# Layer kernel, first batch: weights signal apart, the identity loads alone, GpSimd takes low parts and constants, loads in another order

## The chip, the cores and the metric

One core of one Trainium2 chip runs the kernel. The metric is the device time of one execution in microseconds. The engines are TensorE (PE, with its weight loads as PEld), VectorE (DVE), ScalarE (ACT), GpSimd (POOL) and SyncE (SP), which here only issues DMAs. They run apart and are held together by semaphores.

## The reference, cut to what matters

```python
xn = layernorm(x)                                  # x: 16 x 512 x 256
q, k, v = feature(xn@Wq+bq), feature(xn@Wk+bk), xn@Wv+bv     # elu + 1, 16 heads of 16
kv  = einsum('bkhd,bkhm->bhdm', k, v)
out = einsum('bqhd,bhdm->bqhm', q, kv) / max(sum(q * sum(k)), 1e-6)
attn = out @ Wo + bo
shared = swiglu(xn @ w_in.T) @ w_out.T
g = softmax(xn @ wg.T + gb); e = softmax(masked(xn @ we.T + eb)); top 2 of 8 experts
h = swiglu(xn @ w1.T)
routed = sum over the chosen e of weight[e] * h @ w2[e].T
return x + attn + shared + routed
```

## The kernel before

The program handles the 16 sequences of 512 rows one after the other ("batches"; the first and the last are written out, the 14 between are a hardware loop), and then multiplies the rows, sorted by their pair of experts, with the expert weights. A batch is held transposed as xnT. The order of work on every engine is the order of the code; there is no scheduler.

To keep 32-bit accuracy on an engine that multiplies rounded fp32r numbers, every operand is kept as a high part (rounded to fp32r) and a low part (the rest), and each product is three matmuls (`mm3`: high by high, high by low, low by high). In the first batch all weights must be loaded and split: `high_parts` on ScalarE casts a staged weight and counts `w_round`; `low_parts` on VectorE, or `low_part` and `in_low` on GpSimd, subtracts. VectorE splits W_k, the router's W_r, W_v and W_q and counts `w_split`; GpSimd splits W_in (four times `in_low`, counted by `ffn_split`), the two halves of W_1 (`w1_split`) and W_out. `kv_w_ld` counts the landings of W_k, W_r and W_v together. The staging buffers are kb (W_k, W_v), relut (W_r, then the constants `c_round`), hrow (W_q), res and phiq (W_in), wstage and gated (W_1).

What happens before the first batch's products: VectorE takes the statistics of x, GpSimd the root (`reciprocal_root`, tile rstd), VectorE normalises into hrow (`first_normalise`), TensorE transposes with the identity, which is the first 128 columns of the constant block `c_stay`, ScalarE rounds (`first_high`, xnT_hi) and VectorE subtracts (`first_low`, xnT_lo). TensorE has run 64 matmuls on a constant tile before that (`warm_up`). Then come the constants on VectorE (nbq, triones, spread, run, tok; semaphore `const_set`).

In a batch TensorE does for each of four row tiles the key and router product (6 matmuls) and the value product (6), then the query product, `hidden(0)` (shared expert, chunk 0), the key-value sums, `hidden(1)`, `routed(0)`, ranks, normaliser sums (these need phiq), `routed(1)` to `routed(3)`, the spread of the reciprocals (they need `rdiag`, kept in qn_hi), `hidden(2)`, `hidden(3)` and the output products. VectorE's part: `k_in` adds the key's bias, `phi_k` the feature map, `logits_in`, `probabilities`, `best_two` the routing, then phiq (which in the first batch waits for `ffn_split` to reach 4, since phiq is W_in's staging buffer), `gate(0)`, `gate(1)`, ranks, row tables, reciprocals. In the first batch `stats_in(1)` and `norm_out(1)`, the next batch's statistics, stand among the `k_in`. ScalarE's part: value copies, exponentials, W_1's casts, the query's activations, `silu(0)`, `second_normalise`, W_out's cast, `high(0)` (h_hi), `silu(1)`.

Of the kernel before, what the change touches and what calls it, by code (L numbers as in the profile page):

```python
# [6 lines left out]
def layer_program(nc, x, w_k, w_v, w_q, w_o, w_in, w_out, w_exp, w_rt, b_q, b_kl, b_o,  # L7
# [41 lines left out]
    with ctx:  # L49
# [145 lines left out]
        kv_w_ld = sem("kv_w_ld")  # L195
# [5 lines left out]
        x0_ld = [sem(f"x0_ld{t}") for t in range(TB)]  # L201
        stay_ld = sem("stay_ld")
        c_ld = sem("c_ld")
# [5 lines left out]
        w_split = sem("w_split")  # L209
# [156 lines left out]
        def _(sp):  # L366
# [92 lines left out]
        def _(pe):  # L459
            def first_transposes():  # L460

                pe.wait_ge(stay_ld, 16)
# [33 lines left out]
            def batch(b, last):  # L496

                for t in range(TB):
# [9 lines left out]
                    if first_row(b) and t == 0:  # L508
                        pe.wait_ge(w_split, 2)
# [8 lines left out]
                if first_row(b):  # L518
                    pe.wait_ge(w_split, 3)
# [7 lines left out]
                if first_row(b):  # L527
                    pe.wait_ge(ffn_split, 1)
                    pe.wait_ge(const_set, 1)
# [22 lines left out]

                pe.wait_ge(oh_rdy, b + 1)
# [83 lines left out]
            pe.wait_ge(w_split, 1)  # L637
# [42 lines left out]
        def _(act):  # L680
# [39 lines left out]
            def batch(b, last):  # L720
                if first_row(b):
                    act.wait_ge(w_split, 3)
                    act.wait_ge(const_set, 1)
# [17 lines left out]
                if first_row(b):  # L741
                    act.wait_ge(w1_ld[1], 16)
# [39 lines left out]
            for buf, of, _, _ in stage_kv[1:3]:  # L782
                act.dma_start(buf, of).then_inc(kv_w_ld, 16)
            act.wait_ge(kv_w_ld, 16 * 3)
            high_parts(stage_kv)
# [41 lines left out]
        def _(dve):  # L827
# [155 lines left out]
            def batch(b, last):  # L983
# [153 lines left out]
            def low_parts(stage, n):  # L1137
# [4 lines left out]
                ins.then_inc(w_split, 1)  # L1142
# [21 lines left out]
            low_parts(stage_kv[2:3], 2)  # L1164
            low_parts(stage_q, len(stage_kv))
            dve.wait_ge(c_ld, 16 * 3)
# [250 lines left out]
```

## Time and profile before

| | |
|---|---|
| median of 3 runs | 915.67 us (915.26 to 917.14) |
| the profiled execution, its own time | 917.56 us |
| its span, first to last instruction | 915.6 us |
| TensorE busy | 898.0 us, 98% |
| VectorE / ScalarE / GpSimd busy | 76% / 40% / 44% |
| TensorE's granted clock, mean over the span | 0.993 |

The span lies inside the execution's time; 1.96 us lie around it. A granted clock of 1.00 is TensorE at full speed, 2.4 GHz, and 0.50 at half. Busy times of matmuls overlap a little, as they are pipelined. Times in the rows are counted from the span's start. An "idle before" with an arrow tells how long the engine had stood and what released it.

### The profile page before, as it was taken

Reading aid. Unit: us, or ns where it says so; the run is one execution under the profiler, and the core shown is the slowest. Engines: PE = TensorE matmul, PEld = TensorE weight load, DVE = VectorE, ACT = ScalarE, POOL = GpSimd, SP = SyncE. Lnnn points to the kernel's source line nnn. Section 1 sums busy time; section 2 is a strip of 40 time slices with the busy share of each in tenths; the row PEclk is TensorE's granted clock in tenths of the full one; section 3 lists DMA queues with packets and bytes.
Section 4 is the critical chain, followed back from the end, with each engine's and each line's share of the span. In section 5 each row is a group of like instructions: output and inputs, shape, how many; then the busy total and the mean of one; then the engine's idle time right before and its main releaser. Section 6 shows DMA issues by size and latency. Waiting matters only on the chain. (4 is left out here: it accounts for less than half of the span.)

```text
span 915.6 us, 22781 instructions
## 1 busy us (share of the span) xinstructions
PE 898.0 (98%) x6982; PEld 810.8 (89%) x6983; DVE 694.0 (76%) x1816; ACT 367.3 (40%) x605; POOL 404.0 (44%) x486
## 2 busy tenths in 40 slices
PE   8899999999999999999999999999999999999996
PEld 7698988889898989898898989898988999999996
DVE  6978777787868687877878786878685777777774
ACT  4654534353535445344535354453531222222220
POOL 3654342433434244434343342534341655665554
PEclk9999999999999999999999999999999999999998
DMA  6432414131323323141313233232156888888870
GB/s 215 132 123 70 126 47 126 69 103 70 105 91 102 123 72 117 55 126 69 103 69 103 92 103 109 85 109 65 59 197 140 141 140 144 146 141 150 140 132 1
DMA packets 141992, 98.63 MB, mean 108 GB/s; under 512 B 53136, under 2 KB 133008, under 8 KB 141968
## 3 DMA queue, kind: packets, MB, share of 16 engines
q1 hardware_dynamic: 103584, 62.50, 24.1%
q0 software_dynamic: 15920, 25.32, 12.3%
q10 hardware_dynamic: 22464, 10.51, 5.1%
q8 instruction: 13, 0.21, 0.1%
q14 instruction: 11, 0.09, 0.0%
HBM read 53.29 MB, written 46.43 MB: 109 GB/s over the span
## 5 line engine op out<-in xcount | busy, mean ns | idle before, releaser
L1232 POOL TENSOR_TENSOR h_lo<-gated,h_hi 128x256 fp32r<-128x256 f32 x128 | 98.8, 793 | 139.9 <-ACT h_hi L714 139.9
L355 PE MATMUL bank<-xnT_hi,win_hi 128*128 128x512 f32 x256 | 102.1, 399 | 0.0
L355 PE MATMUL bank<-wone_hi,xnT_hi 128*128 128x512 f32 x256 | 101.5, 397 | 0.2 <-DVE relut L1035 0.2
L356 PE MATMUL bank<-xnT_lo,win_hi 128*128 128x512 f32 x256 | 100.4, 392 | 0.0
L357 PE MATMUL bank<-wone_hi,xnT_lo 128*128 128x512 f32 x256 | 99.7, 390 | 0.0
L356 PE MATMUL bank<-wone_lo,xnT_hi 128*128 128x512 f32 x256 | 99.6, 389 | 0.0
L357 PE MATMUL bank<-xnT_hi,win_lo 128*128 128x512 f32 x256 | 99.6, 389 | 0.0
L1256 POOL TENSOR_TENSOR res<-res,bo_t 128x256 f32<-128x256 f32 x64 | 47.3, 769 | 112.9 <-DMA res<-x 112.9
L1251 POOL DMA_INDIRECT h_d<-hrow,pos_i x64 | 63.1, 986 | 72.8 <-DVE hrow L981 38.3
L355 PE MATMUL bank<-wexp_hi,xnT_hi 128*128 x304 | 85.6, 282 | 2.0 <-DVE xnT_lo L1154 2.0
L356 PE MATMUL bank<-wexp_lo,xnT_hi 128*128 x304 | 85.8, 282 | 0.0
L357 PE MATMUL bank<-wexp_hi,xnT_lo 128*128 x304 | 85.6, 282 | 0.0
L356 PE MATMUL bank<-wexp_lo,h_hi 128*128 x296 | 82.9, 280 | 0.0
L355 PE MATMUL bank<-wexp_hi,h_hi 128*128 x296 | 82.6, 279 | 0.0
L357 PE MATMUL bank<-wexp_hi,h_lo 128*128 x296 | 82.6, 279 | 0.0
L714 ACT CAST h_hi<-gated 128x512 fp32r<-128x512 f32 x64 | 39.7, 621 | 101.3 <-DVE gated L977 101.3
L977 DVE TENSOR_TENSOR gated<-gated,bank 128x512 f32<-128x512 f32 x64 | 43.9, 685 | 47.3 <-ACT gated L710 47.3
L1329 POOL DMA_INDIRECT out<-res,idx_cur x39 | 62.0, 1590 | 36.7 <-DVE res L1183 24.8
L355 PE MATMUL bank<-wout_hi,h_hi 128*128 128x256 f32 x256 | 71.9, 281 | 0.0
L357 PE MATMUL bank<-wout_hi,h_lo 128*128 128x256 f32 x256 | 71.5, 279 | 0.0
L356 PE MATMUL bank<-wout_lo,h_hi 128*128 128x256 f32 x256 | 71.4, 279 | 0.0
L718 ACT ACTIVATE hrow<-bank 128x512 f32<-128x512 f32 x64 | 38.1, 597 | 80.0 <-PE bank L357 80.0
(204 smaller groups left out, 2700.4 us busy)
## 6 DMA issues: line engine op xcount, KB each, us to landing
res<-x SPq DMA_DIRECT2D x16, 512.0 KB, 3.7
out<-res SPq DMA_DIRECT2D x16, 512.0 KB, 2.8
xt<-x SPq DMA_DIRECT2D x15, 512.0 KB, 3.4
xn_d<-xt SPq DMA_DIRECT2D x15, 512.0 KB, 4.9
xt<-xn_d SPq DMA_DIRECT2D x60, 128.0 KB, 2.7
xt<-h_d SPq DMA_DIRECT2D x76, 64.0 KB
xt<-h_d ACTq DMA_DIRECT2D x76, 64.0 KB
kb<-h_d SPq DMA_DIRECT2D x76, 64.0 KB
```

What stands on the lines that cost most here:

```text
L355: e.matmul(to, w_hi, m_hi_, start=first_, stop=False, skip_group_check=free)
L356: e.matmul(to, w_hi, m_lo_, start=False, stop=False, skip_group_check=free)
L357: return e.matmul(to, w_lo, m_hi_, start=False, stop=last_, skip_group_check=free)
L714: act.copy(h_hi[:, j, :], gated[:, j % 2, :]).then_inc(hhi_rdy, 1)
L718: act.activation(hs[t], bank[gate_bank][:, :], ACT.Silu).then_inc(rsil_rdy, 1)
L977: dve.tensor_tensor(gated[:, j % 2, :], gated[:, j % 2, :], bank[up_bank][:, :], ALU.mult).then_inc(gate_rdy, 1)
L1232: ins = pool.tensor_tensor(h_lo[:, j, cols], gated[:, j % 2, cols], h_hi[:, j, cols].bitcast(f32), ALU.subtract)
L1251: pool.indirect_dma_start(d, bass.IndirectOffsetOnAxis(ap=pos_i[:, t:t + 1], axis=0), src, None).then_inc(done, 16)
L1256: ins = pool.tensor_tensor(res[:, t, :], res[:, t, :], bo, ALU.add)
L1329: pool.indirect_dma_start(out, bass.IndirectOffsetOnAxis(ap=idx_cur[:, t // TB, t % TB:t % TB + 1], axis=0), ring[t], None, bounds_check=N ...
```

## The change

Signals: `kv_w_ld` becomes `k_w_ld`, `rt_w_ld` and `v_w_ld`, and ScalarE waits before each cast for its own weight. `w_split` becomes `k_split`, `v_split` and `q_split`. The identity is a load of its own (64 KB, `ident_ld`) in the place of `c_stay`; the other columns follow later.

VectorE subtracts W_k's low part before it normalises, W_r's after. GpSimd subtracts W_v's and W_q's low parts, in halves of 128x256, and makes the five constants, all ahead of W_in's. Its second root now comes behind both halves of W_1.

SyncE waits for the third tile of x before it issues W_q and what follows, and for W_in's landing before it issues W_1. `b_kl` and `b_q` have a signal of their own (`b_ld`). The waits for `const_set` move to later places on TensorE, ScalarE and VectorE. VectorE's `stats_in(1)` comes after the fourth `k_in` instead of the third, and the third waits for `v_split`.

```diff
-            loads(kv_w_ld, [], stage_kv[0:1])
-            sp.dma_start(stay[:, :], c_stay).then_inc(stay_ld, 16)
+            loads(k_w_ld, [], stage_kv[0:1])
+            sp.dma_start(ident, c_stay[:, 0:P]).then_inc(ident_ld, 16)
+            sp.wait_ge(x0_ld[2], 16)
             loads(q_w_ld, [], stage_q)
-            loads(c_ld, [(bkl[:, :], b_kl), (bq[:, :], b_q)], [])
+            loads(b_ld, [(bkl[:, :], b_kl), (bq[:, :], b_q)], [])
+            sp.dma_start(stay[:, P:], c_stay[:, P:]).then_inc(stay_ld, 16)
             loads(in_w_ld, [], stage_in)
...
             sp.dma_start(xt[:, :, :], x_rows(1)).then_inc(x_ld, 16)
+            sp.wait_ge(in_w_ld, 16 * 2)
             for n in range(2):
                 loads(w1_ld[n], [], stage_w1[n:n + 1])
...
-            act.wait_ge(kv_w_ld, 16 * 3)
-            high_parts(stage_kv)
+            for n, done in enumerate((k_w_ld, rt_w_ld, v_w_ld)):
+                act.wait_ge(done, 16)
+                high_parts(stage_kv[n:n + 1])
...
                 for t in range(TB):
+                    if first_row(b) and t == 2:
+                        dve.wait_ge(v_split, 1)
                     k_in(t)
-                    if first_row(b) and t == 2:
+                    if first_row(b) and t == 3:
                         stats_in(1)
-                    if first_row(b) and t == 3:
                         norm_out(1, True)
+                        dve.wait_ge(const_set, 1)
...
             norm(0)
+            low_parts(stage_kv[0:1], 0)
             first_normalise()
-            low_parts(stage_kv[0:2], 0)
+            low_parts(stage_kv[1:2], 1)
             first_low()
...
+            for buf, _, hi, lo, n, done in ((*stage_kv[2], 3, v_split), (*stage_q[0], 4, q_split)):
+                pool.wait_ge(w_round, n)
+                for c in range(DC):
+                    ins = pool.tensor_tensor(lo[:, c, :], buf[:, c, :], hi[:, c, :].bitcast(f32), ALU.subtract)
+                ins.then_inc(done, 1)
+            pool.wait_ge(b_ld, 16 * 2)
+            pool.wait_ge(stay_ld, 16)
...
+            pool.wait_ge(c_ld, 16)
+            pool.tensor_copy(triones[:, 0, :], tri_f)
+            pool.tensor_copy(spread[:, :, :], spread_f).then_inc(const_set, 1)
...
-                if n == 0:
-                    reciprocal_root(1)
+            reciprocal_root(1)
```

GpSimd from the first root to the second, before (win is W_in, wone is W_1):

```order
L1226 TENSOR_TENSOR rstd<-var,mhalf 128x4 [waits var_rdy,pool_set]
L1300 TENSOR_TENSOR win_lo<-res,win_hi 128x128 [waits w_round]
L1300 TENSOR_TENSOR win_lo<-res,win_hi 128x128
L1300 TENSOR_TENSOR win_lo<-phiq,win_hi 128x128 x2
L1300 TENSOR_TENSOR win_lo<-res,win_hi 128x128 x2
L1300 TENSOR_TENSOR win_lo<-phiq,win_hi 128x128 x2
L1291 TENSOR_TENSOR wone_lo<-wstage,wone_hi 128x256 [waits w_round]
L1291 TENSOR_TENSOR wone_lo<-wstage,wone_hi 128x256 x3
L1226 TENSOR_TENSOR rstd<-var,mhalf 128x4 [waits var_rdy]
L1291 TENSOR_TENSOR wone_lo<-gated,wone_hi 128x256 [waits w_round]
L1291 TENSOR_TENSOR wone_lo<-gated,wone_hi 128x256 x3
L1300 TENSOR_TENSOR win_lo<-res,win_hi 128x128 x2
```

And now, the start of the same stretch:

```order
L1231 TENSOR_TENSOR rstd<-var,mhalf 128x4 [waits var_rdy,pool_set]
L1302 TENSOR_TENSOR wv_lo<-kb,wv_hi 128x256 [waits w_round]
L1302 TENSOR_TENSOR wv_lo<-kb,wv_hi 128x256
L1302 TENSOR_TENSOR wq_lo<-hrow,wq_hi 128x256 [waits w_round]
L1302 TENSOR_TENSOR wq_lo<-hrow,wq_hi 128x256
L1306 TENSOR_SCALAR nbq<-bq 128x2 [waits stay_ld,b_ld]
L1307 COPY run<-stay 128x32
L1308 COPY tok<-stay 128x4
L1310 CAST triones<-relut 128x128 [waits c_ld]
L1311 CAST spread<-relut 128x256
L1319 TENSOR_TENSOR win_lo<-res,win_hi 128x128 [waits w_round]
```

Eight instructions for W_v, W_q and constants stand ahead of W_in's low parts, and the constants wait for three loads. The end of the stretch now:

```order
L1296 TENSOR_TENSOR wone_lo<-wstage,wone_hi 128x256 [waits w_round]
L1296 TENSOR_TENSOR wone_lo<-wstage,wone_hi 128x256 x3
L1296 TENSOR_TENSOR wone_lo<-gated,wone_hi 128x256 [waits w_round]
L1296 TENSOR_TENSOR wone_lo<-gated,wone_hi 128x256 x3
L1231 TENSOR_TENSOR rstd<-var,mhalf 128x4 [waits var_rdy]
L1319 TENSOR_TENSOR win_lo<-res,win_hi 128x128 x2
L1319 TENSOR_TENSOR win_lo<-phiq,win_hi 128x128 x2
```

The root has moved behind the second half of W_1, to just ahead of W_in's last two `in_low`.

VectorE from the variance to the constants, before:

```order
L861 TENSOR_SCALAR var<-mv 128x4 [waits v_link]
L870 TENSOR_SCALAR hrow<-xt,mv,rstd 128x256 [waits rstd_rdy]
L870 TENSOR_SCALAR hrow<-xt,mv,rstd 128x256 x3
L1141 TENSOR_TENSOR wk_lo<-kb,wk_hi 128x2x256 [waits w_round]
L1141 TENSOR_TENSOR wk_lo<-relut,wk_hi 128x2x10 [waits w_round]
L883 TENSOR_TENSOR xnT_lo<-bank,xnT_hi 128x512 [waits thi] x2
L1141 TENSOR_TENSOR wv_lo<-kb,wv_hi 128x512 [waits w_round]
L1141 TENSOR_TENSOR wq_lo<-hrow,wq_hi 128x512 [waits w_round]
L1169 TENSOR_SCALAR nbq<-bq 128x2 [waits stay_ld,kv_w_ld,c_ld]
L1170 CAST triones<-relut 128x128
L1171 CAST spread<-relut 128x256
```

And now, down to the first `k_in` (kb):

```order
L872 TENSOR_SCALAR var<-mv 128x4 [waits v_link]
L1154 TENSOR_TENSOR wk_lo<-kb,wk_hi 128x2x256 [waits w_round]
L881 TENSOR_SCALAR hrow<-xt,mv,rstd 128x256 [waits rstd_rdy]
L881 TENSOR_SCALAR hrow<-xt,mv,rstd 128x256 x3
L1154 TENSOR_TENSOR wk_lo<-relut,wk_hi 128x2x10 [waits w_round]
L894 TENSOR_TENSOR xnT_lo<-bank,xnT_hi 128x512 [waits thi] x2
L999 TENSOR_TENSOR kb<-bank,bkl 128x256 [waits stay_ld,k_done,b_ld,k_split]
```

W_k's low part has moved ahead of the normalisation, and W_v, W_q and the constants are gone from the engine. VectorE around the second statistics, before:

```order
L988 TENSOR_TENSOR kb<-bank,bkl 128x256 [waits k_done]
L989 TENSOR_TENSOR lg<-bank,bkl 128x10
L988 TENSOR_TENSOR kb<-bank,bkl 128x256 [waits k_done]
L989 TENSOR_TENSOR lg<-bank,bkl 128x10
L850 BN_STATS stats<-xt 128x6 [waits x_ld]
L850 BN_STATS stats<-xt 128x6 x3
L988 TENSOR_TENSOR kb<-bank,bkl 128x256 [waits k_done,v_link]
L989 TENSOR_TENSOR lg<-bank,bkl 128x10
L857 BN_AGGR mv<-stats 128x2 x4
```

And now:

```order
L999 TENSOR_TENSOR kb<-bank,bkl 128x256 [waits k_done,v_split]
L1000 TENSOR_TENSOR lg<-bank,bkl 128x10
L999 TENSOR_TENSOR kb<-bank,bkl 128x256 [waits k_done]
L1000 TENSOR_TENSOR lg<-bank,bkl 128x10
L861 BN_STATS stats<-xt 128x6 [waits x_ld]
L861 BN_STATS stats<-xt 128x6 x3
L868 BN_AGGR mv<-stats 128x2 [waits v_link]
L868 BN_AGGR mv<-stats 128x2 x3
```

The four statistics stand behind the fourth key addition. SyncE's issues, before:

```order
L372 DMA kb<-w_k 128x512
L374 DMA stay<-c_stay 128x443
L372 DMA hrow<-w_q 128x512
L372 DMA bkl<-b_kl 128x266
L372 DMA bq<-b_q 128x2
L372 DMA res<-w_in 128x1024
L372 DMA phiq<-w_in 128x1024
L372 DMA relut<-c_round 128x384
L380 DMA xt<-x 128x4x256 [waits xn_rdy]
L372 DMA wstage<-w_exp 128x1024
```

And now:

```order
L378 DMA kb<-w_k 128x512
L380 DMA stay<-c_stay 128x128
L378 DMA hrow<-w_q 128x512 [waits x0_ld2]
L378 DMA bkl<-b_kl 128x266
L378 DMA bq<-b_q 128x2
L384 DMA stay<-c_stay 128x315
L378 DMA res<-w_in 128x1024
L378 DMA phiq<-w_in 128x1024
L378 DMA relut<-c_round 128x384
L388 DMA xt<-x 128x4x256 [waits xn_rdy]
L378 DMA wstage<-w_exp 128x1024 [waits in_w_ld]
L378 DMA gated<-w_exp 128x1024
```

The first load of `stay` is the identity, the second the rest; W_in (res, phiq) goes behind a wait and two more issues, W_1 behind a wait for W_in.

## Rows read from the trace of the kernel before

**Rows 1.** The page, part 1: busy us (share of the span) xinstructions.
```profile
PE 898.0 (98%) x6982; PEld 810.8 (89%) x6983; DVE 694.0 (76%) x1816; ACT 367.3 (40%) x605; POOL 404.0 (44%) x486
```

**Rows 2.** Windows: stretch, PE, PEld, DVE, ACT, POOL busy (x), PEclk, DMA share, GB/s.
```profile
10.70:11.88 1.18, 1.10 (x7) 0.91 (x7) 1.18 (x3) 0.21 (x1) 0.00 (x0) 0.88 1.02 381
...
14.00:15.00 1.00, 1.00 (x6) 1.00 (x6) 0.49 (x3) 0.74 (x1) 0.18 (x1) 0.50 1.02 414
15.00:16.00 1.00, 1.00 (x10) 1.00 (x9) 0.39 (x2) 0.20 (x1) 1.00 (x3) 1.00 0.98 374
...
40.00:60.00 20.00, 18.44 (x124) 16.58 (x123) 15.71 (x32) 5.98 (x10) 13.38 (x17) 1.00 0.28 100
```

**Rows 3.** Timeline, TensorE: start us, us, instruction, idle before and its releaser.
```profile
7.99 1.09 PE L466 MATMUL bank<-stay,hrow 128*128 128x128 f32 x8 [1.45 <-DMA stay<-c_stay]
...
10.78 0.36 PE L355 MATMUL bank<-wk_hi,xnT_hi 128*128 128x266 f32 x1 [1.70 <-DVE xnT_lo L883]
...
17.59 0.29 PE L357 MATMUL bank<-wk_hi,xnT_lo 128*128 128x266 f32 x1
...
31.41 0.64 PE L569 MATMUL bank<-phiq,khead 128*32 128x128 f32 x16 [0.73 <-DVE phiq L1022]
...
43.17 0.73 PE L593 MATMUL bank<-qn_hi,spread 128*128 128x512 f32 x2 [1.56 <-DVE qn_hi L1065]
```

**Rows 4.** Timeline, ScalarE: casts, and h_hi of the first hidden chunk.
```profile
8.18 0.62 ACT L683 CAST wk_hi<-kb 128x512 fp32r<-128x512 f32 x1 [4.26 <-DMA kb<-w_v]
...
12.75 1.04 ACT L683 CAST win_hi<-res 128x1024 fp32r<-128x1024 f32 x1 [1.84 <-DMA phiq<-w_in]
...
32.67 0.61 ACT L714 CAST h_hi<-gated 128x512 fp32r<-128x512 f32 x1
```

**Rows 5.** Timeline, VectorE, from normalising to gate 1.
```profile
6.67 1.38 DVE L870 TENSOR_SCALAR hrow<-xt,mv,rstd 128x256 f32<-128x256 f32 x4 [1.25 <-POOL rstd L1226]
...
9.94 1.29 DVE L883 TENSOR_TENSOR xnT_lo<-bank,xnT_hi 128x512 fp32r<-128x512 f32 x2 [0.33 <-ACT xnT_hi L688]
...
13.19 0.17 DVE L1169 TENSOR_SCALAR nbq<-bq 128x2 f32<-128x2 f32 x1 [0.77 <-DMA relut<-c_round]
...
16.46 0.42 DVE L988 TENSOR_TENSOR kb<-bank,bkl 128x256 f32<-128x256 f32 x1 [1.07 <-PE bank L357]
...
19.36 1.23 DVE L995 SCALAR_TENSOR_TENSOR hrow<-kb,hrow 128x512 f32<-128x512 f32 x1
...
29.52 1.29 DVE L1022 TENSOR_TENSOR phiq<-hrow,relut 128x512 f32<-128x512 f32 x2
...
31.22 0.68 DVE L977 TENSOR_TENSOR gated<-gated,bank 128x512 f32<-128x512 f32 x1
...
33.81 0.69 DVE L977 TENSOR_TENSOR gated<-gated,bank 128x512 f32<-128x512 f32 x1 [1.34 <-ACT gated L710]
```

**Rows 6.** Timeline, GpSimd, the weights' low parts and the second root.
```profile
14.82 0.88 POOL L1300 TENSOR_TENSOR win_lo<-res,win_hi 128x128 fp32r<-128x128 f32 x2 [8.18 <-ACT win_hi L683]
...
21.85 1.04 POOL L1226 TENSOR_TENSOR rstd<-var,mhalf 128x4 f32<-128x4 f32 x1
...
23.30 2.83 POOL L1291 TENSOR_TENSOR wone_lo<-gated,wone_hi 128x256 fp32r<-128x256 f32 x4 [0.41 <-ACT wone_hi L683]
...
28.60 0.88 POOL L1300 TENSOR_TENSOR win_lo<-phiq,win_hi 128x128 fp32r<-128x128 f32 x2
```

**Rows 7.** SyncE's issues from the timeline, then W_k's us to landing.
```profile
1.66 0.42 SPq L372 DMA_DIRECT2D kb<-w_k  x1
...
4.02 0.74 SPq L372 DMA_DIRECT2D res<-w_in  x1
...
kb<-w_k SPq DMA_DIRECT2D x1, 256.0 KB, 3.8
```

**Rows 8.** One line's instructions: duration ns min/median/max, first and last start.
```profile
L1141 DVE TENSOR_TENSOR wv_lo<-kb,wv_hi x1: 679/679/679, 11.1 to 11.1; 128x512 fp32r<-128x512 f32 x1
...
L1291 POOL TENSOR_TENSOR wone_lo<-wstage,wone_hi x4: 732/738/1179, 18.6 to 21.2; 128x256 fp32r<-128x256 f32 x4
```

More of the change, by code:

```diff
@@ L192, in layer_program @@
         bank = [ctx.enter_context(nc.psum_tensor(f"bank{i}", [P, 512], f32)) for i in range(8)]
-        kv_w_ld = sem("kv_w_ld")
+        k_w_ld = sem("k_w_ld")
+        rt_w_ld = sem("rt_w_ld")
+        v_w_ld = sem("v_w_ld")
         q_w_ld = sem("q_w_ld")
@@ L201, in layer_program @@
         x0_ld = [sem(f"x0_ld{t}") for t in range(TB)]
+        ident_ld = sem("ident_ld")
         stay_ld = sem("stay_ld")
+        b_ld = sem("b_ld")
         c_ld = sem("c_ld")
@@ L208, in layer_program @@
         w_round = sem("w_round")
-        w_split = sem("w_split")
+        k_split = sem("k_split")
+        v_split = sem("v_split")
+        q_split = sem("q_split")
         ffn_split = sem("ffn_split")
@@ L460, in first_transposes @@
             def first_transposes():
-                pe.wait_ge(stay_ld, 16)
+                pe.wait_ge(ident_ld, 16)
                 for t in range(TB):
@@ L508, in batch @@
                     if first_row(b) and t == 0:
-                        pe.wait_ge(w_split, 2)
+                        pe.wait_ge(v_split, 1)
                     if t == 2:
@@ L518, in batch @@
                 if first_row(b):
-                    pe.wait_ge(w_split, 3)
+                    pe.wait_ge(q_split, 1)
                 for o in range(DC):
@@ L528, in batch @@
                     pe.wait_ge(ffn_split, 1)
-                    pe.wait_ge(const_set, 1)
                 wait(pe, base_rdy, DC * b)
@@ L551, in batch @@
                 routed(0, (3, 4))
+                if first_row(b):
+                    pe.wait_ge(const_set, 1)
                 pe.wait_ge(oh_rdy, b + 1)
@@ L636, in _ @@
             first_transposes()
-            pe.wait_ge(w_split, 1)
+            pe.wait_ge(k_split, 2)
             rounds(pe, batch, B)
@@ L721, in batch @@
                 if first_row(b):
-                    act.wait_ge(w_split, 3)
-                    act.wait_ge(const_set, 1)
+                    act.wait_ge(q_split, 1)
                 for i in range(2):
@@ L741, in batch @@
                 if first_row(b):
+                    act.wait_ge(const_set, 1)
                     act.wait_ge(w1_ld[1], 16)
@@ L781, in _ @@
                 act.dma_start(xt[:, t, :], x[0, t * P:(t + 1) * P, :]).then_inc(x0_ld[t], 16)
-            for buf, of, _, _ in stage_kv[1:3]:
-                act.dma_start(buf, of).then_inc(kv_w_ld, 16)
-            act.wait_ge(kv_w_ld, 16 * 3)
-            high_parts(stage_kv)
+            for (buf, of, _, _), done in zip(stage_kv[1:3], (rt_w_ld, v_w_ld)):
+                act.dma_start(buf, of).then_inc(done, 16)
+            for n, done in enumerate((k_w_ld, rt_w_ld, v_w_ld)):
+                act.wait_ge(done, 16)
+                high_parts(stage_kv[n:n + 1])
             first_high()
@@ L1141, in low_parts @@
                     ins = dve.tensor_tensor(lo, buf, hi.bitcast(f32), ALU.subtract)
-                ins.then_inc(w_split, 1)
+                ins.then_inc(k_split, 1)
             def transposed(t, g):
@@ L1160, in _ @@
             norm(0)
+            low_parts(stage_kv[0:1], 0)
             first_normalise()
[L1162 removed]
+            low_parts(stage_kv[1:2], 1)
             first_low()
[L1164 to L1167 removed]
+            dve.wait_ge(k_split, 2)
+            dve.wait_ge(b_ld, 16 * 2)
             dve.wait_ge(stay_ld, 16)
[L1169 to L1175 removed]
             rounds(dve, batch, B)
@@ L1292, in low_part @@
                 ins.then_inc(done, 1)
+            for buf, _, hi, lo, n, done in ((*stage_kv[2], 3, v_split), (*stage_q[0], 4, q_split)):
[5 more added lines that the diff above has]
+            pool.wait_ge(stay_ld, 16)
+            pool.tensor_scalar(nbq[:, :], bq[:, :], -1.0, None, ALU.mult)
+            pool.tensor_copy(run[:, :], slot_row)
+            pool.tensor_copy(tok[:, :], tok0)
+            pool.wait_ge(c_ld, 16)
+            pool.tensor_copy(triones[:, 0, :], tri_f)
+            pool.tensor_copy(spread[:, :, :], spread_f).then_inc(const_set, 1)
             first = len(stage_kv) + len(stage_q)
```

8 lines of the change are left out of this document (removed).

## The prediction

> **What bounds the kernel now.** First the busy shares: TensorE is busy 898.0 of the 915.6 us, nothing else above 76% [rows 1]. So a change saves time only where TensorE stands or runs slowly. Next the windows over the first 60 us, where the change is, for TensorE's busy time and granted clock [rows 2]. From 10.70 to 11.88 us the clock averages 0.88, which is full speed followed by about 0.28 us at half, so it fell near 11.6. From 14 to 15 us it is still 0.50, the 1.2 GHz level, and from 15 us 1.00 again, 2.4 GHz. That is 3.4 us at half speed, a loss of 1.7 us. TensorE had stood 1.45 us before the transposes and 1.70 us before the first key product. From 40 to 60 us it misses 1.56 us, all before 43.17. TensorE's rows name its waits [rows 3]: the identity's load until 7.99, xnT_lo until 10.78, phiq until 31.41, rdiag (qn_hi) until 43.17, the last for 1.56.
>
> The other three engines tell what sets the last two. Read backwards: TensorE at 43.17 follows VectorE, which has had no idle time to speak of since gate 1 at 33.81. That waited 1.34 us for ScalarE's second silu, and before the silu stand, without a gap, its second normalisation, W_out's cast and h_hi (32.67) [rows 4, 5]. ScalarE's own chain began when VectorE's logits came, and these follow phi_k at 19.36 after an unbroken 2.90 us from the third key addition at 16.46 [rows 5]. Beside it runs GpSimd: low parts from 14.82 to 29.48, with one root between them at 21.85, and phiq starts at 29.52, as it waits for the last of them [rows 5, 6]. Two chains thus end together at phiq, and a third, ScalarE's, has 0.8 us of slack (gate 0, 1.7 us after phiq starts, is done at 31.9; h_hi runs at 32.67). TensorE's own earlier start is worth nothing until both yield.
>
> **The change part by part.** The sum goes against the profiled execution, 917.56 us (span 915.6); the runs' median, 915.67, is 1.89 us below it, and I carry differences over.
>
> 1. *Key low part ahead of normalising.* W_k is issued at 1.66 and lands 3.8 us later, 5.5 [rows 7]. The cast takes 0.62 [rows 4] and the subtraction 0.68, by the same form on W_v [rows 8]; they end near 6.85, and normalising started at 6.67 [rows 5]. Price: +0.2, last tile near 8.2 instead of 8.05.
> 2. *Identity alone, separate weight signals.* The transposes no longer wait for 221 KB; they follow the normalised tiles. The last two (0.14 each, 1.09 for eight [rows 3]) end near 8.55 instead of 9.08. ScalarE has its three casts behind it, since W_k, W_r and W_v no longer share one signal (it idled 4.26 us until 8.18 [rows 4]). So xnT_hi and then xnT_lo start 0.8 us earlier, 9.15 for 9.94, and the first key product at 10.0 for 10.78 [rows 3, 5]. Gain on TensorE: 0.8.
> 3. *W_v and W_q low parts to GpSimd.* A half (128x256) takes 0.74, so 1.5 us a matrix against 0.68 on VectorE [rows 8]. W_v: from about 7.6 to 9.1, wanted at 10.9. W_q: cast after xnT_hi, about 9.6 to 10.2; low part until 11.8, wanted after 15.8 at the earliest. Both cost nothing here. The Trainium skill ("GPSIMD Engine Reference", Engine selection) says that two-input elementwise work belongs on VectorE, GpSimd being about twice as slow. The rows agree (1.5 to 0.68), and the rule would price the move at 1.6 us, if GpSimd were not idle then; the trace shows it idle for 8.18 us before 14.82 [rows 6].
> 4. *Constants to GpSimd.* VectorE no longer waits for c_round until 13.19 [rows 5]. Of GpSimd's five instructions two wait for c_round, near 13.5, and none is larger than the 0.74 us form above, so they end by 15.0 at the latest. Nothing else on it is due before W_in's high parts, now 14.8 [rows 6]. Bounds: 0, and 1 us if c_round is that much later.
> 5. *Loads.* W_q, b_kl, b_q, the rest of c_stay and W_in leave after the third x tile has landed (about 4.0, an estimate), so that W_in, issued at 4.02 now [rows 7], goes about 1.9 us later. Bytes ahead of W_in's end are the same, and the DMA engines carry 381 and 414 GB/s in the windows around it [rows 2], so I move its landing from 12.7 [rows 4] only to 13.0; bounds: 12.4 (fewer transfers at once) and 14.6 (all 1.9 us kept). ScalarE's casts then end at 15.0. W_1's two loads, now behind W_in, land near 16.8 and 18 (3.4 to 3.9 us after W_in, an estimate from W_k's 3.8); ScalarE comes to the first near 16.8, so no cost.
> 6. *Stats after the fourth key addition.* phi_k(0) now comes one addition, four statistics and the aggregation (2.90 minus 0.45, 2.45 us) after the fourth key product, not 2.90 after the third. The 42 products up to there end at 17.88, 7.1 us after the first began, with the loss of 1.7 in them: 5.4 at full clock [rows 3].
> 7. *Root after both W_1 low parts.* The 1.04 us stood in a gap, as W_1's second high part was ready only 0.41 us after it [rows 6]. Now it stands on the chain to phiq. Price: up to 1.0.
>
> What the clock does decides. The idle time before the first key product falls from 1.70 to about 1.4 us and that before the transposes from 1.45 to 0.8, so I take it that the clock stays up, a little likelier than not. The Trainium skill ("TensorE: Matmul & The Clock Gate", HAM oscillation) has standing between bursts as the cause of the fall and warns that each costs the next burst. By that rule shorter gaps should spare the loss; where they still fall under it, the rival below holds. The trace shows one fall here and cannot say how near it was.
>
> *Clock stays up:* fourth key product at 10.0 + 5.4 = 15.4; phi_k(0) 17.85, 1.5 earlier. ScalarE's second W_1 cast ends 21.75. GpSimd: 15.0 + 3.4 (half of W_in, as from 26.1 to 29.48) + 3.1 = 21.5; then 21.8 + 2.83 + 1.04 + 3.4 = 29.1 [rows 6], so phiq 0.4 earlier. Gate 0 ends 31.5, h_hi runs at 31.5 for 32.67, and gate 1 at 32.65 for 33.81. Of 2.5 us on TensorE (0.8 + 1.7) 1.15 remain at 43.17; the rest stands as longer waits before phiq and rdiag. After that TensorE has no gap to give it back in, so it reaches the end.
>
> The runs may not have met the fall at all (they lie 1.89 below the profiled one). Without it the kernel before has phi_k(0) near 17.7 and phiq near 29.1 by the same working, so the gain would be nothing. Between 0 and 1.15 I take 0.6, 915.67 less 0.6: 915.1, with 914.3 to 915.8 as its own range.
>
> **The rivals.**
> *The clock falls again.* The fourth key product ends at 10.0 + 7.1 = 17.1, phi_k(0) at 19.55, 0.2 later than now; W_1's second cast 23.45, and with the root behind it GpSimd ends at 30.7, phiq 1.2 later. Of this the slack of 0.8 takes most: about 0.5 slower, 916.2. For: 1.4 us of standing is still there. Against: less of it.
> *All of it arrives.* W_in lands at 12.4, so that GpSimd's chain is through at 28.5, and phi_k, which took 1.23 us at 19.36 beside GpSimd [rows 5], takes the 0.68 of a subtraction of its size. Then VectorE's and ScalarE's chain is 1.5 + 0.55 earlier and all of that reaches 43: 2.05 less, 913.6. For: the clock's 1.7 us and the front's 0.8 are there to be had. Against: GpSimd's rows leave it 0.4.
> *Slower: GpSimd's chain.* It decides once W_in's high parts end after about 15.8 (W_in at 13.8) or GpSimd's instructions stretch beside VectorE's (one half-size took 1.18 instead of 0.74, rows 8). From there each us is a us on phiq, gate 0 and gate 1. With W_in at 14.6 and one such stretch, 2.0 us later than in the forecast: 1 to 1.8 slower, 917.1.
> *It does nothing:* the front's 0.8 us vanish in the waits for phiq and rdiag and the rest cancels: 915.7.
>
> **How the numbers follow.** Forecast 0.46, clock falls again 0.19, all of it 0.12, slower chain 0.10, nothing 0.13. A measurement of this kernel tells about 0.2%, 1.8 us, from no change: below 913.8 is faster, above 917.5 slower. The third case and a tail of the first give 0.14 faster; the slower chain's upper half and a tail of the second 0.07; 0.79 within. The range 913.5 to 916.8 leaves out about half of each outer case.
>
> **What would show it.** Right: transposes ending near 8.6, first key product near 10.0, W_in's casts ending near 15, GpSimd's root after W_1's low parts, VectorE standing before phiq until near 29, qn_hi's product near 42. The clock of 11 to 15 us tells forecast from first rival. Wrong: W_in landing past 13.8, normalising held by W_k beyond 7.2, a longer wait at 43 than 1.56 plus 1.2, or TensorE gaps after 45 us that differ.

## The result, and the profile after

The changed kernel takes 918.64 us (median of 12 runs, 914.87 to 919.71), the kernel before 915.72 on the same chip (12 runs, 915.09 to 917.27): ratio 1.0028, interval 1.0017 to 1.0039. It is slower, 1.8 us above the range's upper end. Two more measurements of it gave 918.99 (1.0035 [1.0015, 1.0056]) and 918.51 (1.0011 [0.9995, 1.0026]). Now and then a run of any kernel takes under 912.7 us; means and shares below leave these out, as well as two runs of the kernel before of 1788 and 5042 us, and the last section comes back to the short ones.

The profiled execution has a span of 917.0 us for 915.6. The busy shares hardly move [rows 1]; page, part 1:

```profile
PE 898.4 (98%) x6982; PEld 809.8 (88%) x6983; DVE 695.1 (76%) x1809; ACT 367.6 (40%) x605; POOL 408.3 (45%) x495
```

Windows of TensorE (stretch, length, busy, clock, DMA share, GB/s), to be held against [rows 2]:

```profile
30.00:40.00 10.00, 7.45 (x43) 0.83 0.62 180
...
40.00:60.00 20.00, 20.00 (x130) 1.00 0.23 83
```

The fall near 11.6 us is gone (11.88 to 14 has clock 1.00), but there is a new one at 33.28, 3.41 us long. From 40 to 60 us TensorE no longer stands at all: what was a wait of 1.56 us has in this trace become TensorE's own lateness. Its timeline, as [rows 3]:

```profile
7.49 0.67 PE L475 MATMUL bank<-stay,hrow 128*128 128x128 f32 x4 [0.36 <-DVE hrow L881]
8.45 0.44 PE L475 MATMUL bank<-stay,hrow 128*128 128x128 f32 x2 [0.29 <-DVE hrow L881]
9.18 0.44 PE L475 MATMUL bank<-stay,hrow 128*128 128x128 f32 x2 [0.29 <-DVE hrow L881]
11.00 0.36 PE L361 MATMUL bank<-wk_hi,xnT_hi 128*128 128x266 f32 x1 [1.38 <-DVE xnT_lo L894]
...
30.59 0.22 PE L565 MATMUL bank<-oh,triones 128*128 128x128 bf16 x1 [1.02 <-DVE oh L957]
32.70 0.65 PE L579 MATMUL bank<-phiq,khead 128*32 128x128 f32 x16 [1.75 <-DVE phiq L1035]
...
43.99 0.81 PE L603 MATMUL bank<-qn_hi,spread 128*128 128x512 f32 x2
```

TensorE has its identity in time, but each pair of transposes now waits for VectorE's normalising. VectorE, as [rows 5]:

```profile
6.32 0.69 DVE L1154 TENSOR_TENSOR wk_lo<-kb,wk_hi 128x512 fp32r<-128x512 f32 x1 [0.84 <-ACT wk_hi L693]
6.93 2.19 DVE L881 TENSOR_SCALAR hrow<-xt,mv,rstd 128x256 f32<-128x256 f32 x4
9.05 0.17 DVE L1154 TENSOR_TENSOR wk_lo<-relut,wk_hi 128x20 fp32r<-128x20 f32 x1
10.16 1.29 DVE L894 TENSOR_TENSOR xnT_lo<-bank,xnT_hi 128x512 fp32r<-128x512 f32 x2 [0.95 <-ACT xnT_hi L698]
...
19.00 0.51 DVE L872 TENSOR_SCALAR var<-mv 128x4 f32<-128x4 f32 x1
19.42 1.03 DVE L1006 SCALAR_TENSOR_TENSOR hrow<-kb,hrow 128x512 f32<-128x512 f32 x1
...
30.81 1.29 DVE L1035 TENSOR_TENSOR phiq<-hrow,relut 128x512 f32<-128x512 f32 x2 [0.36 <-POOL win_lo L1319]
```

The four normalising instructions take 2.19 us for 1.38, and GpSimd, idle there before, runs W_v's low part beside them. GpSimd, as [rows 6]:

```profile
7.41 1.56 POOL L1302 TENSOR_TENSOR wv_lo<-kb,wv_hi 128x256 fp32r<-128x256 f32 x2 [0.73 <-ACT wv_hi L693]
...
15.00 0.29 POOL L1310 CAST triones<-relut 128x128 bf16<-128x128 f32 x1 [1.86 <-DMA relut<-c_round]
...
16.49 0.89 POOL L1319 TENSOR_TENSOR win_lo<-res,win_hi 128x128 fp32r<-128x128 f32 x2 [0.85 <-ACT win_hi L693]
...
23.58 2.83 POOL L1296 TENSOR_TENSOR wone_lo<-gated,wone_hi 128x256 fp32r<-128x256 f32 x4
26.38 1.03 POOL L1231 TENSOR_TENSOR rstd<-var,mhalf 128x4 f32<-128x4 f32 x1
```

ScalarE's casts, as [rows 4], with the loads that released them:

```profile
5.67 0.62 ACT L693 CAST wk_hi<-kb 128x512 fp32r<-128x512 f32 x1 [1.76 <-DMA kb<-w_k]
...
14.41 1.05 ACT L693 CAST win_hi<-res 128x1024 fp32r<-128x1024 f32 x1 [3.27 <-DMA phiq<-w_in]
...
33.22 0.62 ACT L724 CAST h_hi<-gated 128x512 fp32r<-128x512 f32 x1 [0.60 <-DVE gated L988]
```

W_k's own signal frees ScalarE 2.5 us earlier; W_in comes 1.7 later. Where the lost time stays is seen at the second batch, whose first m_hi follows TensorE's kv sums. ScalarE, before and then after:

```profile
85.76 0.59 ACT L769 CAST m_hi<-bank 128x512 fp32r<-128x512 f32 x1 [0.27 <-PE bank L588]
```

```profile
86.52 0.59 ACT L779 CAST m_hi<-bank 128x512 fp32r<-128x512 f32 x1 [0.27 <-PE bank L598]
```

Each later batch takes 42.14 us in both, up to 676 us. In three traces of the changed kernel this cast starts at 86.52, 86.96 and 86.81, in two of the kernel before at 85.76 and 85.39: 1.2 us apart on average.

What TensorE waits for on the way there is seen at the spread of the reciprocals, which needs qn_hi from VectorE. VectorE's line before, the changed kernel's in its first trace, and both engines' in its second (after_again):

```profile
42.42 0.69 DVE L1065 TENSOR_TENSOR qn_hi<-relut,stay 128x512 fp32r<-128x512 f32 x1
```

```profile
42.40 0.69 DVE L1078 TENSOR_TENSOR qn_hi<-relut,stay 128x512 fp32r<-128x512 f32 x1
```

```profile
43.65 0.69 DVE L1078 TENSOR_TENSOR qn_hi<-relut,stay 128x512 fp32r<-128x512 f32 x1
...
44.40 0.73 PE L603 MATMUL bank<-qn_hi,spread 128*128 128x512 f32 x2 [0.70 <-DVE qn_hi L1078]
```

In the first trace VectorE is through as early as before, at 43.09, and TensorE comes 0.9 us later; in the second TensorE waits for VectorE.

### The profile page after: what moved, and what is told of

It is laid out like the page before. It is cut to its first block and busy times, and to the rows that moved or that the text cites. A ratio compares the mean times of both kernels' runs of the same rounds, so it can differ in the third digit from the quotient of the medians.

```text
span 917.0 us, 22788 instructions
## 1 busy us (share of the span) xinstructions
PE 898.4 (98%) x6982; PEld 809.8 (88%) x6983; DVE 695.1 (76%) x1809; ACT 367.6 (40%) x605; POOL 408.3 (45%) x495
```

## The experiments

Eighteen more runs follow, three of them of the two kernels unchanged, each of five rounds unless said. "Offset" is a kernel's median less that of the kernel before in the same job, so that chips compare; the interval is that of the ratio.

**after_again, after_third (three rounds), before_again.** Both kernels once more, unchanged.

> The changed kernel, unchanged. Theory loads and root: W_in's cast between 14 and 15 and phiq near 30.8 again, time 2 to 3 us above before_again. Rival chance: W_in's cast anywhere between 12.5 and 14.5 (root_between, with the same loads, had 12.84), and phiq with it.

> The changed kernel, unchanged, for a third trace. In the first two m_hi of the second batch came at 86.52 and 86.96 (before 85.76 and 85.39), normalising took 2.19 and 2.29, W_in's cast came at 14.41 and 13.64. Theory sharing: normalising above 2.1 and m_hi between 86.2 and 87.2 again, time 2.5 to 3 above before. Rival chance: normalising near 1.38, m_hi near 85.5.

> The kernel before, unchanged, for a second trace of it and for times on one chip with the next three. The first traces gave W_in's cast at 12.75 and phiq at 29.52 for it. Theory loads and root (the change lengthens GpSimd's chain): phiq between 29 and 30 again. Rival chance (the two traces differed because transfers land differently in each execution, not by the change): W_in's landing moves here by 1 us or more without a change, and phiq with it.

Changed: 918.99 and 918.51, offsets +3.0 and +2.2. Before: 916.52 beside 915.95, 1.0004 [0.9983, 1.0026]. Of 157 runs of the kernel before 51, a third, have a mean granted clock of 0.997 or more. The four traces with such a clock (before_again, before_fillers and two more with fillers) have no fall while TensorE works, the sixteen others at least one, so I take these runs to have had none. Of 32 of the changed kernel none has such a clock. At 0.996 or less the kernel before takes 916.9 us on average, the changed one 918.6: some 1.7 us are its own, and the rest is that a fall has become certain. In before_again, without a fall at 11.6, phi_k(0) starts at 19.21 and phiq at 29.17, not 17.7 and 29.1 as I had worked out. The two small instructions ahead of phi_k(0) explain 1.1 us of that, with GpSimd beside them in both traces of the kernel before. VectorE in the first trace, then in before_again:

```profile
19.13 0.25 DVE L860 TENSOR_SCALAR nmean<-mv 128x4 f32<-128x4 f32 x1
19.29 0.16 DVE L861 TENSOR_SCALAR var<-mv 128x4 f32<-128x4 f32 x1
```

```profile
17.90 0.70 DVE L860 TENSOR_SCALAR nmean<-mv 128x4 f32<-128x4 f32 x1
18.51 0.79 DVE L861 TENSOR_SCALAR var<-mv 128x4 f32<-128x4 f32 x1
```

So stretching beside GpSimd is no invention of the change: it differs from one execution of the kernel before to the next, by up to 1.1 us here. The third changed trace has W_in's cast 0.5 earlier than the first and yet phiq 0.5 later. GpSimd there:

```profile
24.06 2.83 POOL L1296 TENSOR_TENSOR wone_lo<-gated,wone_hi 128x256 fp32r<-128x256 f32 x4 [1.41 <-ACT wone_hi L693]
26.84 1.05 POOL L1231 TENSOR_TENSOR rstd<-var,mhalf 128x4 f32<-128x4 f32 x1
```

It stood 1.41 us for ScalarE's second W_1 cast (22.95), which waits its turn behind the exponentials of the logits (22.81), which wait for VectorE behind phi_k (20.05). So the chain comes from the key products, not from W_in; then comes the root. In the first trace GpSimd had no gap, as W_in was latest there.

**loads_as_before.** The changed kernel with the loads in the old order.

```diff
-            sp.wait_ge(x0_ld[2], 16)
+            sp.dma_start(stay[:, P:], c_stay[:, P:]).then_inc(stay_ld, 16)
...
-            sp.wait_ge(in_w_ld, 16 * 2)
```

> The changed kernel (918.6 us) with the loads in the order of before: identity, rest of the constants, W_q, biases, W_in, c_round, no wait for x or for W_in. Theory loads: W_in landed at 14.40 instead of 12.75, so GpSimd's chain to phiq started 1.65 later (16.49 for 14.82) and ended 1.3 later; with W_in back at 12.8 phiq starts near 29.2 instead of 30.81, TensorE's wait before it shrinks from 1.75 to below 0.5, and the time falls by 1.3 to 3 us, the larger figure if the clock then doesn't fall near 33: 915.6 to 917.3. Theory sharing (GpSimd's low parts beside VectorE): the time stays within 0.7 of 918.6, as VectorE's routing chain, whose one-hot ended 0.9 later, holds TensorE all the same. Theory clock alone: as loads, since it needs the shorter waits.

918.99, 1.0019 [0.9998, 1.0041], offset +2.6, though W_in is cast at 12.41: as a whole the old order brings nothing back. For W_in's landing alone it is no clean test. The old order also makes W_k late (cast at 6.55 for 5.67, so that normalising starts at 7.81 and the first key product at 11.88), and this trace has two stretches at the lower clock ahead of 40 us, one of 6.8 us. But phiq, at 32.85, is the latest of all with W_in among the earliest, so there W_in is not what it waits for.

**lows_on_vector.** W_v's and W_q's low parts back on VectorE.

```diff
+            low_parts(stage_kv[2:3], 2, v_split)
+            low_parts(stage_q, 3, q_split)
...
-            for buf, _, hi, lo, n, done in ((*stage_kv[2], 3, v_split), (*stage_q[0], 4, q_split)):
...
```

> The changed kernel with W_v's and W_q's low parts back on VectorE behind xnT_lo, constants still on GpSimd. Theory sharing: normalising took 2.19 us beside W_v's low part instead of 1.38; without it the transposes end near 8.8 instead of 9.62 and the first key product starts near 10.2 instead of 11.00; if this front counts, the time falls by 0.8 or more, to 917.8 or less. Theory loads: GpSimd still waits for W_in's high parts until 16.4, phiq stays near 30.8, so the time stays 918.6 within 0.5 although the first key product moves by 0.8.

917.07, 0.9998 [0.9979, 1.0018], offset +0.7: about 2 us back. Normalising takes 1.38 again. The profiled execution shows less than that: W_k came late in it, the first key product starts at 10.80, phiq at 30.68, and m_hi of batch 2 at 85.97.

**root_between.** The second root between W_1's halves.

```diff
-            reciprocal_root(1)
+                if n == 0:
+                    reciprocal_root(1)
```

> The changed kernel with the second root back between the two halves of W_1. GpSimd ran from 16.49 to 30.77 without a gap of note, W_1's second cast was ready at 23.08 and its low part began at 23.58, so the root costs the same 1.04 at either place. All theories on loads and clock: phiq unchanged within 0.3, time 918.6 within 0.5. Against it my step 7 (the root behind both halves costs up to 1.0): the time falls by 0.5 to 1.0.

917.92, 1.0004 [0.9986, 1.0022], offset +1.6; phiq starts at 29.46. The root costs about 1 us, within what the runs can just tell. In this trace normalising still takes 2.20 us and the first key product starts at 11.39, yet m_hi of batch 2 is at 85.64, within the two of the kernel before. So the stretch alone need not cost anything; but no fall of the clock stands ahead of batch 2 here, and the trace can't part that from the root.

**before_fillers (nine runs).** The kernel before with more products on the constant tile, so that TensorE stands less before the transposes and the first key product.

```diff
-    WARM = 64
+    WARM = 84
...
+            warm_up(24)
```

> The kernel before with 84 instead of 64 warm-up products and 24 more after the transposes, so that TensorE hardly stands before the first key product; results unchanged. It measures what the clock's fall at 11.6 costs before. Theory clock: the kernel before runs in two groups (915.1 to 915.8 and 916.3 to 917.3) by whether the clock falls in the front; with the fillers all runs fall in the lower group, median 915.2 or below, at most 1.5 less. Rival: the fall is hidden by GpSimd's chain, and the two groups stay: median 915.7 within 0.3.

914.54, 0.9970 [0.9959, 0.9981], offset -1.8: faster than both kernels. No fall is in its trace while TensorE works, and phiq starts at 27.94. W_in is cast at 11.40, 1.0 to 1.35 us ahead of the kernel before's two traces, and nothing in the edit touches the loads.

**lows_and_root_back.** The edits of lows_on_vector and root_between together.

> The changed kernel with W_v's and W_q's low parts back on VectorE and the second root back between the halves of W_1; signals, identity, constants and loads stay changed. With lows_on_vector 917.07 and root_between 917.92 on one chip where before ran 916.35: if sharing and the root are the two costs and add, this is within 0.7 of before_again. If the loads are the cost (W_in landing late), it stays 1 us or more above before_again and phiq is past 30.

917.81, 1.0018 [0.9998, 1.0038], offset +1.9: worse than lows_on_vector alone, inside the intervals. It doesn't separate the two. By what I had written ahead, this offset and phiq at 30.26 speak for the loads.

**three_back.** These two and the loads of loads_as_before.

> The changed kernel with low parts of W_v and W_q on VectorE, the root between the halves of W_1 and the loads as before: left of the change are the split signals, the identity alone, W_k's low part ahead of normalising, the constants on GpSimd and the statistics after the fourth key addition. Theory: late W_in, sharing and root were the cost and the rest is near neutral: W_in's cast 12.2 to 12.8, phiq 29.0 to 29.6, time within 0.7 of before in the same job. Rival (statistics and W_k's place cost too): first key product still at 10.7 to 11, phi_k past 19.6, 1 us or more above before.

917.01, 1.0015 [1.0001, 1.0029], offset +0.6, with phiq at 29.69. It is lower than lows_and_root_back, again inside the intervals; before_new_loads, below, says the opposite of the loads.

**signals_only.** three_back, and besides W_k's low part behind normalising and the statistics after the third key addition; separate signals and the identity's load are left of the change.

```diff
-            low_parts(stage_kv[0:1], 0)
             first_normalise()
+            low_parts(stage_kv[0:1], 0)
...
-                    if first_row(b) and t == 3:
+                    if first_row(b) and t == 2:
                         stats_in(1)
```

> As three_back, and W_k's low part behind normalising, statistics after the third key addition: left are signals, identity alone and GpSimd's constants. Theory: normalising starts at 6.7 and the transposes end near 8.6, so the first key product starts at 10.0 to 10.2 against 10.78 and 10.94 before; phiq is then set by GpSimd (W_in), so at most 0.5 faster than before. Rival: the front counts, 0.8 or more faster.

916.45, 0.9994 [0.9974, 1.0014], offset 0. The first key product starts at 9.90, 0.9 us earlier than before, and m_hi at 41.60 for 41.65: this part alone is harmless and worth nothing, as the clock falls at 11.18 and phi_k(0) is at 19.26.

**key_and_stats_back.** The changed kernel with only those last two edits.

> The changed kernel with W_k's low part behind normalising and the second statistics after the third key addition. Between three_back (917.01) and signals_only (916.45) these two were worth 0.6. Theory: worth the same here, 0.4 to 1.0 less than the changed kernel, since normalising starts at 6.7 instead of 6.9 to 7.3 but still overlaps W_v's low part; if the last two key additions wait for the statistics, 0. Rival (W_k's landing, 5.7 to 6.6 in five traces, is what holds the front): 1.5 or more.

918.33, 1.0017 [1.0001, 1.0032], offset +1.5. W_v's low part starts 1.1 us behind the start of normalising, not 0.3 to 0.5 as in the changed kernel. Normalising takes 1.38, and here the stretch falls on GpSimd's first instruction and on the small one behind W_k's low part. One line's instructions (duration ns min/median/max, start), and VectorE's, of this kernel:

```profile
L1303 POOL TENSOR_TENSOR wv_lo<-kb,wv_hi x2: 720/1090/1459, 7.7 to 9.2; 128x256 fp32r<-128x256 f32 x2
```

```profile
7.90 0.68 DVE L1155 TENSOR_TENSOR wk_lo<-kb,wk_hi 128x512 fp32r<-128x512 f32 x1
8.50 0.73 DVE L1155 TENSOR_TENSOR wk_lo<-relut,wk_hi 128x20 fp32r<-128x20 f32 x1
```

m_hi of batch 2 is at 85.80, 1.0 us earlier than in the changed kernel.

**wv_after_normalise.** The changed kernel, but GpSimd starts W_v's low part only when VectorE has normalised all four tiles.

```diff
+            pool.wait_ge(xn_rdy, TB)
```

> The changed kernel, but GpSimd waits for the four normalised tiles before W_v's low part, so that the two do not run side by side; nothing else moved. Theory sharing (normalising stretched from 1.38 to 2.2 us beside W_v's low part, which makes the key products late): normalising takes 1.38 again, the transposes end 0.8 earlier, the first key product starts near 10.2 to 10.7, and the time falls by 1.5 to 2.2 against the changed kernel, to 0.7 to 1.4 above before. Rival (the low parts on GpSimd cost by holding GpSimd itself, its chain to phiq): the front moves by 0.8 and the time by less than 0.4.

917.72, 1.0009 [0.9990, 1.0027], offset +0.8: one wait brings back 2 of the 2.9 us by the medians, though this interval overlaps the changed kernel's (1.0017 to 1.0039). The trace agrees: m_hi of batch 2 is at 85.17 for 86.5 to 87.0. VectorE's normalising, first in the changed kernel, then in this one:

```profile
L881 DVE TENSOR_SCALAR hrow<-xt,mv,rstd x4: 408/608/819, 6.9 to 8.3; 128x256 f32<-128x256 f32 x4
```

```profile
L881 DVE TENSOR_SCALAR hrow<-xt,mv,rstd x4: 407/408/409, 6.6 to 7.6; 128x256 f32<-128x256 f32 x4
```

The longest takes 819 ns for 408, and all are back at 408 once GpSimd is held off. W_v's low part, 8.09 to 9.50, is still in time, and the first key product starts at 9.89, where I had forecast it. W_k was cast 0.3 us earlier than in the changed kernel's first trace, which is part of that.

**after_fillers.** The changed kernel with 46 such products ahead of its wait for the one-hot rows.

```diff
+                    for _ in range(46):
+                        pe.matmul(bank[5][:, 0:P], triones[:, 1, :], triones[:, 1, :], start=True, stop=True)
```

> The changed kernel with 46 small products in the first batch ahead of the wait for the one-hot, where TensorE stood 1.02 and 1.75 us before the clock fell at 33.28. Theory clock: the clock stays up from 30 to 40, the first batch's m_hi comes at 42.7 instead of 44.38, and the time falls by 1 to 1.7 us against after_again. Rival: the chains on the other engines set the pace up to 45 us, so the fall costs nothing and the time is that of after_again within 0.4.

916.52, 1.0013 [0.9995, 1.0030], offset +0.6. Its trace has a fall at 10.89 and none near 33; m_hi of batch 1 is at 43.35 for 44.38. But the product on qn_hi starts at 44.00, waiting 0.68 us for VectorE, where the first changed trace has it at 43.99, and m_hi of batch 2 is at 86.56, no earlier. So the gain does not stand in the first batch, and without the fall the other engines' chain sets the same pace. The rival was right on the pace and not on the time, which fell by 2 us.

**after_front_fillers.** The changed kernel with WARM at 76 and 24 products behind the transposes.

> The changed kernel with 12 more warm-up products and 24 after the transposes, so the clock should not fall before 15 us. Worth 1.8 in the kernel before and 2.0 in signals_only; with 46 later fillers instead the changed kernel gained 2.5. Theory clock: the fall near 11 (in four of seven traces of changed variants) is part of the changed kernel's loss, and the gain is 1 to 2. Rival (in the changed kernel GpSimd's chain sets phiq whatever the front does, and the clock falls later, near 33): gain below 0.5, and a fall at 32 to 35 in the trace.

916.41, 0.9999 [0.9990, 1.0007], offset -0.5. The fall at 34.44 is there and m_hi of batch 2 at 86.58, no earlier than in the changed kernel. So its gain does not stand in the first batch either.

**before_new_loads.** The kernel before with SyncE's two new waits alone.

```diff
+            sp.wait_ge(x0_ld[2], 16)
...
+            sp.wait_ge(in_w_ld, 16 * 2)
```

> The kernel before with the changed waits on SyncE alone: the third x tile ahead of W_q, and W_in ahead of W_1. Theory loads: W_in's cast between 13.3 and 14.5 instead of 12.4 to 12.8, GpSimd's chain and phiq 1.0 to 1.6 later (30.2 to 31.2), time 0.7 to 1.5 above before. Rival (loads as before changed nothing in the changed kernel, 918.99, so the loads do not count): within 0.5 of before.

915.50, 0.9995 [0.9979, 1.0011], offset -0.9. The new loads do not hurt; whether they help the runs don't tell.

**signals_fillers, signals_fillers_new_loads, new_loads_fillers.** WARM 76 and 24 products added to signals_only, to that with the changed loads, and to before_new_loads.

> As signals_only, with 12 more warm-up products and 24 after the transposes. The kernel before with fillers ran 914.54 where before ran 916.35. Theory clock: the clock stays up in the front and through the waits for phiq, the time is 1.5 to 2.2 below before, as low as before_fillers or 0.3 lower. Rival: fillers gained by chance of W_in's landing (11.40 in that trace): the gain is below 0.7.

> signals_fillers with the changed order of loads and SyncE's two waits. The kernel before with the two waits alone ran 915.50 against 916.42. Theory (fewer loads in flight land W_k, W_v and the identity earlier, and W_in is not late by itself): 0.3 to 1.0 below signals_fillers, that is 2.2 to 3.0 below before. Rival (W_in at 13.0 to 14.4 in the traces with the changed loads lengthens GpSimd's chain): 0.5 to 1.3 above signals_fillers.

> The kernel before with SyncE's two new waits (alone 0.7 to 0.9 below before) and with 12 more warm-up products and 24 after the transposes (alone 1.8 below). If the two add, 2.3 to 2.7 below before in the same job, the fastest version so far; if both only keep TensorE's clock up in the front, no better than the fillers alone, 1.8 below.

914.44 (0.9978 [0.9960, 0.9997]), 915.00 (0.9979 [0.9969, 0.9989]) and 914.63 (0.9985 [0.9974, 0.9995]), offsets -2.0, -1.9 and -1.7. All beat both kernels, and none beats before_fillers (-1.8) by what can be told: neither the separate signals nor the loads add to the fillers' gain.

## Why the prediction was wrong

**The step that failed is the third, "Both cost nothing here".** It placed W_v's low part rightly (7.41 to 8.97 for 7.6 to 9.1) and asked only whether GpSimd was idle. It did not ask what VectorE was doing meanwhile: normalising, on the path to the first key product. The four tiles took 2.19 to 2.29 us in all three traces of the changed kernel for 1.38, so the last transposes end at 9.62 instead of 8.55 and the first key product starts at 11.0 to 11.4 instead of 10.0. Held apart, they take 1.38 and it starts at 9.89; that and taking the work off GpSimd each bring back about 2 us by the medians, with intervals that overlap the changed kernel's. That VectorE's stretch is real, and goes when GpSimd is held off, is shown; how much of the 2.9 us it is, less surely, as root_between was no slower at batch 2 with the stretch in it. The Trainium skill ("SBUF — State Buffer", SBUF: two separate sides) says that VectorE and GpSimd share a port pair which one instruction holds to its end, while the other is blocked; on VectorE's side it names instructions with two SBUF inputs or in a two-port mode. The rows fit: single instructions of 408 ns take up to 819 beside GpSimd (893 in the third trace), and in key_and_stats_back GpSimd's first one takes 1459 for 727 beside W_k's low part, and VectorE's 128x20 one 729 for 170. Whether normalising runs in such a mode no run shows. I had the stretch in hand [rows 8], and used it only for GpSimd's own chain in a rival.

- *Key low part ahead of normalising (+0.2):* right in the first trace, normalising at 6.93 for 6.67; 7.20 and 7.13 in the others, as W_k was cast 0.2 to 0.3 later. Three_back and signals_only differ by 0.6 us with overlapping intervals, for this and the statistics together.
- *Identity and signals (-0.8):* right by itself, 9.90 in signals_only, and worth nothing in the end.
- *Constants (0):* c_round came at 15.0, not 13.5, but W_in's high parts later still; right.
- *Loads (13.0, bounds 12.4 to 14.6):* 14.41, 13.64 and 13.94; mis-sized by about 1 us inside the bounds. Its price the runs don't settle: loads_as_before got nothing back, before_new_loads lost nothing, and three_back lies below lows_and_root_back. SyncE's issue of W_in was 1.9 us later, as forecast.
- *Statistics (2.45 us behind the fourth key product):* 2.89 from the fourth key addition to phi_k(0) (16.53 to 19.42), 3.56 and 3.23 in the other two traces. The small instructions stretch beside GpSimd: var takes 0.51, 0.78 and 0.79 for 0.16. The term was too small by 0.4 to 1.1, as I had it from a trace without that stretch; before_again has it too.
- *Root ("up to 1.0"):* 1.03 on the chain; right at its bound. My working had let other gains cover it. For the low parts ahead of it I put 3.1 us where the trace I worked from has 3.28; they took 3.76, 2.81 and 3.28.
- *The clock:* it did stay up at 11.6 in two of the three traces. But the waits grew elsewhere: 1.02 for the one-hot rows and 1.75 for phiq, 2.50 in one piece in the third trace. Behind them the clock is at its lower level, 1.2 GHz, from 33.3 on for 3.4 us. "The clock decides" was not right: the fall was near 33, at 11.6 and near 33 in the three traces, and m_hi of batch 2 came at 86.52, 86.96 and 86.81 all the same. The product on qn_hi starts at 43.99, 44.40 and 44.29 for 43.17 and 42.81. The fall near 33 holds it up by 0.9 us in the first trace and 0.3 in the third, and in the second nothing but VectorE does; VectorE is ready at 43.09, 44.34 and 44.00, for 43.11 and 42.76 before. The fall at 11.6 had been nearly hidden: before_again, without it, has m_hi of batch 1 at 41.29 for 41.65. The trace I worked from has a second fall, near 694.3, which my windows of the first 60 us did not reach.
- *The rivals:* the slower GpSimd chain had the right side, the stretch and the place: phiq 30.8 to 31.6 for 29.5, price 1 to 1.8 (917.1). The measured 918.6 is above it. Its condition, W_in past 13.8, held in two of the three traces, but the one with 13.64 has the latest phiq, so it does not decide. I had given this rival 0.10.

Of the signs I named, the later first key product was the first to show the error; "a longer wait at 43" failed as a sign, because in the first trace TensorE itself was late there.

**Open.** The traces account for 1.4 to 1.6 us of span, the medians for 2.2 to 3.0. The fall that a third of the runs were spared, some 1.2 us each, explains 0.4 of it; about 1 us I have not located. Nor do I know why all kernels with fillers have a shorter second stage (last batch's m_hi to TensorE's end). It is 229.0 to 229.7 us in the six of them and 230.3 to 232.0 in the others, short runs apart:

| kernel | offset | m_hi of batch 2 | second stage |
|---|---|---|---|
| before, two traces | | 85.76, 85.39 | 231.3, 231.1 |
| changed, three traces | +2.2 to +3.0 | 86.52, 86.96, 86.81 | 231.9, 231.1, 231.3 |
| wv_after_normalise | +0.8 | 85.17 | 231.4 |
| root_between | +1.6 | 85.64 | 232.0 |
| signals_only | 0 | 85.35 | 232.0 |
| signals_fillers | -2.0 | 85.32 | 229.4 |
| after_fillers | +0.6 | 86.56 | 229.7 |
| after_front_fillers | -0.5 | 86.58 | 229.4 |
| before_fillers | -1.8 | 83.81 | 229.0 |

In three of the four rows with fillers the whole gain stands in the second stage, none ahead of batch 2. TensorE's wait there, in before_again and then in before_fillers:

```profile
692.30 0.38 PE L355 MATMUL bank<-wexp_hi,xnT_hi 128*128 x1 [1.35 <-DVE xnT_lo L1154]
```

```profile
692.87 0.38 PE L355 MATMUL bank<-wexp_hi,xnT_hi 128*128 x1 [0.30 <-DVE xnT_lo L1155]
```

Products in the first 11 us can't directly shorten a wait at 692. So the fillers' gain is measured, but it is not shown to come from the clock in front: of these only before_fillers is earlier at batch 2, and its W_in landed 1.0 us or more earlier. No run tried fillers that leave the clock as it is.

## What to carry to other kernels

"That engine is idle then" is half of the question when VectorE's work goes to GpSimd: look also at what VectorE runs in those same microseconds, and if it is on the path, hold GpSimd back until it is done. A wait that a change lengthens can also move a fall of the clock; what the fall costs depends on whether another engine's chain ends as late anyway, as it did in two of three traces here. Take two or three traces of the kernel before ahead of the sum: two small instructions that took 0.2 us in one took 1.3 in the other. When one gate on a path is removed (the identity's load), name the next one, and check that another edit of the same change does not make it later.

## What the runs showed of the hardware

Filler products at the start, which compute nothing, lowered every kernel that got them: the changed one by 3.4 us (offset -0.5 for +2.9), signals_only by 2.0, the kernel before by 1.8, before_new_loads by 0.8. Where that gain stands in the traces is told under "Open"; why is not known. The same load of W_in was cast at 12.75 and 12.39 in two executions of one kernel and at 14.41, 13.64 and 13.94 in three of the other. With the edits that leave the loads alone the spread is wider, 11.40 (before_fillers) to 12.75 and 12.84 (root_between) to 14.41: a landing is known to about 1.5 us at best.

Falls of the clock in front of the second stage stand only behind the three longest waits for its first product: 2.02 us (the kernel before), 2.12 (root_between) and 1.89 (signals_only), and behind none of the waits of 0.3 to 1.7 us in the other traces.

The rare short runs (12 of 169 of the kernel before, 909 to 912 us) are not the clock's. Windows of TensorE in the second stage, of such a run (lows_and_root_back, span 909.4) and of before_again:

```profile
780.00:800.00 20.00, 20.00 (x179) 1.00 0.87 150
```

```profile
780.00:800.00 20.00, 20.00 (x172) 1.00 0.89 148
```

At the same granted clock 179 matmuls pass in 20 us instead of 172, and the second stage takes 222 to 223 us for 231. Three of the profiles show it; why is open.
